# Decoder kernel on one core: who issues the loads of the row maxima, when the class rows are stored, and where the router products stand

## The chip, the cores and the metric

The kernel runs on one core of one Trainium2 chip. The metric is the device time of one execution in microseconds (us); three executions of the kernel before are given, and one more was recorded by the hardware profiler.

## The reference

The program is a two-layer decoder on x of 4 batches x 512 tokens x 128 channels (16 heads of 8 channels). Each line adds a block's output to x:

```python
x = x + L0_attn(_layernorm(x), ...)                  # rwkv, a scan
x = x + L0_xattn(_layernorm(x), ctx_1024, ...)
x = x + L0_ffn(_layernorm(x), ...)                   # causal attention + FFN, and experts
x = x + L1_attn(_layernorm(x), ...)                  # attention with relative positions
x = x + L1_xattn(_layernorm(x), ctx_1024, ...)
x = x + L1_ffn(_layernorm(x), ...)                   # grouped attention
```

The change lies in the third and the sixth. In the third:

```python
scores = jnp.einsum('bqhd,bkhd->bhqk', q, k) / np.sqrt(hd)
attn = softmax(where(causal, scores, min)); o = attn @ v
...
probs = softmax(xt @ router_w); topw, topi = top_k(probs, 2)   # 8 experts
moe_out = sum of topw * expert(xt) over the two chosen
```

In the sixth a similarity with a guide vector puts each token in one of two classes, and softmax attention runs over the keys of the query's own class:

```python
sim = (sim - sim.min()) / (sim.max() - sim.min()); pos = sim > 0.9
x_pos = masked_attn(pos); x_neg = masked_attn(~pos)
reg_out = (x_pos[:, :REG] + x_neg[:, :REG]) * 0.5        # the first 5 tokens
tok_out = where(pos, x_pos[:, REG:], x_neg[:, REG:])
```

## The kernel before

The stages follow one another with a barrier between them. `attention_stage` (L518) is called twice: with the tag `da` for the causal attention of the third block (with `gates`, the router's work, woven in) and with `ga` for the grouped attention of the sixth (with `classes` and `front`, the work on classes and on the first tokens). Both go through 16 units of four heads of one batch, and 8 steps each: 128 steps, written out as loops over `step` on each engine. The order on an engine is the order of its code; semaphores are the only link between the engines.

Exact fp32 scores are made from bf16 parts. Queries and keys are split in three bf16 parts (`parts`), written to DRAM (`stacks_dram`, L606) and loaded again in another layout as `qst` and `kst` (L628), for one unit at a time, into one of NBUF = 4 buffers. For batch 0 SP (SyncE) writes and loads by units (`write_quad`, `load_stack`); the other three batches are written whole (`write_parts`, 18 DMAs) before the loads of the units 4 to 15.

In step n:

- PE (TensorE) makes the scores of step n (L730; in `da` L741 adds the causal mask), DVE (VectorE) reduces them to row maxima (L964). At the end of a unit DVE splits the unit's maxima in three bf16 parts (L947 to L953). In step 8u + 9 PE turns them into rows (`turn_maxima`, L750), ACT (ScalarE) copies the rows to `mrows` (`copy_maxima`, L880) and raises `m_ready`, and two DMAs put them below the queries in `qst` (`load_maxima`, L886), so that the maximum is subtracted by the product itself.
- Thirteen steps later (S_LAG) PE makes the transposed scores (`scores_t`, L765), of a new unit u in step 8u + 13 and after `m_loaded`; ACT takes the exponentials (L872); in `da` POOL (GpSimd) clears what the causal mask excludes (L681); three steps later PE multiplies by the values (`values`, L784), and ACT copies a finished unit out (L892).

The score banks form a ring of two, so PE can be two score steps ahead of DVE; the transposed scores have three banks, and L765 waits for ACT's exponentials of the step before.

`gate_programs` holds the router: `route` (L1060) makes 16 products of 128 tokens with the router's weights (L1063; two passes each, so 32 MATMULs), `chain` is DVE's work on them: its first instruction copies the logits out of bank 6 (L1094), the others come from step 24 on. `grouped_front` is the front of `ga`: on DVE it makes the class rows (`rows_made`, L2306 to L2312), and `store_classes` (L2380) stores them in DRAM with four DMAs, waits for these, and `load_classes` (L635) loads them for a unit with four. `registers_pe` (L2145) puts the work on the first tokens in the steps 3 to 12: L2151 turns what POOL has divided by the totals (L2370).

Of the kernel before, what the change touches and what calls it, by code (L numbers as in the profile page):

```python
# [517 lines left out]
def attention_stage(nc, g, tag, xn, wq, wk, wv, group, scale, o, wo, take, patch=None, causal=False, classes=None,  # L518
# [6 lines left out]
    S_LAG, V_LAG = 13, 3  # L525
    GATE_STEP = 24

# [26 lines left out]
    with ExitStack() as ctx:  # L554
# [9 lines left out]
        with ExitStack() as inner:  # L564
# [32 lines left out]
            with nc.Block() as block:  # L597
                @block.sync
                def _(sp):
# [38 lines left out]

                    for u in range(NBUF):
                        write_quad(u)  # L640
                        if u:
                            load_stack(u - 1)
                    load_stack(NBUF - 1)
                    if front:
                        front.store_classes(sp)
                        for u in range(NBUF):
                            load_classes(u)
                    for b in range(1, B):
                        write_parts(b)
                    for u in range(NBUF, QUADS):  # L650
                        load_stack(u)
                        if classes:
                            load_classes(u)
                    for b in range(1, B):
# [30 lines left out]
                def _(pe):  # L685
# [21 lines left out]
                    else:  # L707
                        project()
                        clear_output()
                    if gates:  # L710
                        gates.route(pe)
                    pe.wait_ge(left, 2 * B)
# [98 lines left out]
                    for step in range(ALL_STEPS):  # L811
                        t = step - S_LAG
                        if step < STEPS:
                            scores(step)
                        if 0 <= t < STEPS:
                            scores_t(t)
                        if causal and step < STEPS:
                            mask_scores(step)
                        if step % 8 == 1 and step // 8 - 1 in turn_slot:
                            turn_maxima(step // 8 - 1)  # L820
                        if 0 <= t - V_LAG < STEPS:
                            values(t - V_LAG)
                        if front and step < S_LAG:
                            front.registers_pe(pe, step)
                        if front and step == S_LAG - 1:
                            clear_output()
                        if step in OUT_STEP:
                            output(OUT_STEP[step])
                        if step in JOIN_STEP:
                            join(JOIN_STEP[step])  # L830
                        if gates and step == S_LAG:
                            pe.wait_ge(gates.copied, 1)
# [8 lines left out]
                def _(act):  # L841
# [40 lines left out]

                    def load_maxima(u):
                        act.wait_ge(m_ready, u + 1)
                        for par in range(2):
                            act.dma_start(qst[64 * par + KS:64 * par + KT, u % NBUF, :, :],  # L886
                                          mrows[6 * par:6 * par + 6, u % 2, :]).then_inc(m_loaded[u % 2], 16)

# [8 lines left out]
                    for step in range(ALL_STEPS):  # L897
                        t = step - S_LAG
                        if front and step < S_LAG:
                            front.registers_act(act, step)  # L900
                        if 0 <= t < STEPS:
                            exponentials(t)
                        if step % 8 == 1 and step // 8 - 1 in turn_slot:
                            copy_maxima(step // 8 - 1)
                            load_maxima(step // 8 - 1)
                        if gates and step == GATE_STEP + 6:
                            gates.exp(act)
                        p = t - V_LAG
                        if p >= 0 and p % 8 == 7:
                            copy_output(p // 8)  # L910
# [10 lines left out]
                def _(dve):  # L921
# [33 lines left out]
                    chain = gates.chain(dve) if gates else None  # L955
                    if gates:
                        next(chain)
                    for step in range(STEPS):
                        u, r = divmod(step, 8)
                        pr, qt = divmod(r, 4)  # L960
                        if gates and step >= GATE_STEP:
                            next(chain, None)
# [77 lines left out]
class gate_programs:  # L1040
# [18 lines left out]

    def route(self, pe):  # L1060
        pe.wait_ge(self.g.weights_loaded[3], 16)
        for n in range(self.tiles):
            last = self.nc.tensor.matmul(self.logits[:, n, :], self.xn[:, n // QT, bass.ts(n % QT, 128)],  # L1063
                                         self.g.w("router"), start=True, stop=True)
        last.then_inc(self.routed, 1)
# [23 lines left out]
    def chain(self, dve):  # L1089
        nc, p, hot1, hot2, rank, most = self.nc, self.p, self.hot1, self.hot2, self.rank, self.most  # L1090
        spread = most[:, :].unsqueeze(2).broadcast_to([128, self.tiles, E])
        order = self.g.c("order").unsqueeze(1).broadcast_to([128, self.tiles, E])
        dve.wait_ge(self.routed, 1)
        nc.vector.tensor_copy(p[:, :, :], self.logits).then_inc(self.copied, 1)  # L1094
# [945 lines left out]
class grouped_front:  # L2040
# [339 lines left out]
    def store_classes(self, sp):  # L2380
        sp.wait_ge(self.rows_made, 6)
        for b in range(B):
            sp.dma_start(self.rows_dram[:, b, :], self.rows[32 * b:32 * b + 1, :, :]).then_inc(self.rows_stored, 16)
        sp.wait_ge(self.rows_stored, 16 * B)

# [147 lines left out]
```

## Time and profile before

| | us |
|---|---|
| median of 3 runs | 1348.95 |
| lowest, highest | 1347.19, 1350.35 |
| the profiled execution's own time | 1349.48 |
| its span, first to last instruction | 1347.8 |
| busy PE, DVE, ACT, POOL | 1129.5, 833.1, 730.6, 331.8 |
| mean granted clock of TensorE, as a share of 2.4 GHz | 0.931 |
| stage `da`, from its first stack write to its last output copy | 196.7 to 402.6 |
| stage `ga`, from its first stack write to the last add | 1099.1 to 1341.5 |

The table gives the profiled execution's numbers unless it says otherwise. In the rows below a time is in us from the span's start, `ACTq` and `SPq` are the instructions that issue DMAs, `x2` after a row says how many instructions it merges, and in brackets stand the engine's idle time before it and what ended it (`issue`: nothing that the profile shows). `L886` is line 886 of the kernel printed above.

### The profile page before, as it was taken

How to read it: one execution, taken by the hardware profiler on the slowest of the kernel's cores; microseconds unless marked ns; L12 is line 12 of the kernel's file. 1: busy time of each engine (PE TensorE's matmuls, PEld its weight loads, DVE VectorE, ACT ScalarE, POOL GpSimd, SP SyncE). 2: the span in 40 equal slices, each digit the busy share in tenths (PEclk: the TensorE clock that was granted, in tenths of full speed). 3: DMA queues.
4: the chain of work that ended last, by engine and by line, in shares of the span. 5: the costliest groups of instructions: out<-in, count | busy, mean ns of one | idle time of the engine just before them, and what ended most of it. 6: DMA issues, size and time to landing. Idle time of an engine off the chain costs nothing. (4 is left out here: it accounts for less than half of the span.)

```text
span 1347.8 us, 35730 instructions
## 1 busy us (share of the span) xinstructions
PE 1129.5 (84%) x14748; PEld 565.2 (42%) x14748; DVE 833.1 (62%) x1316; ACT 730.6 (54%) x1439; POOL 331.8 (25%) x664
## 2 busy tenths in 40 slices
PE   5987788777777999568999999999978866888886
PEld 2332333323323444235766666766745333222221
DVE  3997136766653333336776776776736366888884
ACT  4201453666653222546676676776754362788884
POOL 1543021333320333014422324222204413000000
PEclk8998776999997999779999999999999887899999
DMA  4000007111005330033102102010110022311100
GB/s 179 1 0 0 1 21 227 39 39 38 27 3 105 82 62 1 0 120 41 11 8 17 9 8 18 9 11 7 10 8 1 0 54 90 120 39 39 39 15 32
DMA packets 134480, 51.62 MB, mean 38 GB/s; under 512 B 103904, under 2 KB 126448, under 8 KB 133680
## 3 DMA queue, kind: packets, MB, share of 16 engines
q1 hardware_dynamic: 133744, 48.95, 15.5%
q8 instruction: 118, 1.93, 0.6%
q10 hardware_dynamic: 576, 0.39, 0.1%
q14 instruction: 42, 0.34, 0.1%
HBM read 33.12 MB, written 15.81 MB: 36 GB/s over the span
## 5 line engine op out<-in xcount | busy, mean ns | idle before, releaser
L1952 DVE TENSOR_REDUCE re_nmax<-ps 128x1 f32<-128x512 f32 x256 | 159.0, 684 | 88.6 <-PE ps L1720 88.6
L1863 ACT ACTIVATE re_p<-ps,re_nmax 128x512 f32<-128x512 f32 x256 | 158.9, 688 | 89.9 <-DVE re_nmax L1952 89.9
L964 DVE TENSOR_REDUCE ga_nmax<-ps 128x2 f32<-128x1024 f32 x128 | 149.8, 1219 | 28.4 <-PE ps L730 28.3
L872 ACT ACTIVATE ga_pt<-ps 128x512 f32<-128x512 f32 x256 | 139.2, 598 | 38.3 <-issue 22.0
L1741 PE MATMUL ps<-const,re_p 128*128 128x128 f32 x1024 | 145.3, 281 | 8.0 <-ACT re_p L1863 5.2
L964 DVE TENSOR_REDUCE da_nmax<-ps 128x2 f32<-128x256 f32 (+3 forms) x128 | 103.7, 822 | 46.9 <-PE ps L741 45.3
L872 ACT ACTIVATE da_pt<-ps 128x512 f32<-128x512 f32 (+3 forms) x256 | 97.6, 438 | 60.8 <-PE ps L765 35.4
L1741 PEld LDWEIGHTS ps<-const,re_p 128*128 128x128 f32 x1024 | 108.8, 141 | 36.7 <-ACT re_p L1863 25.3
L1869 ACT ACTIVATE re_pT<-ps 128x512 f32<-128x512 f32 x128 | 76.3, 597 | 28.2 <-PE ps L1741 19.7
L784 PE MATMUL ps<-ga_pt,ga_v 128*9 128x256 f32 x1024 | 81.4, 386 | 10.1 <-ACT ga_osum L892 10.1
L1972 DVE COPY re_pT<-ps 128x512 f32<-128x512 f32 x128 | 82.3, 685 | 10.2 <-PE ps L1741 9.4
L1235 DVE TENSOR_TENSOR ex_u<-ps,ex_s 128x512 f32<-128x512 f32 x48 | 33.2, 691 | 89.6 <-PE ps L1208 89.6
L681 POOL TENSOR_SCALAR_AFFINE_SELECT da_pt<-da_pt 128x256 f32<-128x256 f32 x128 | 52.8, 412 | 143.3 <-ACT da_pt L872 141.8
L1221 ACT ACTIVATE ex_s<-ps 128x512 f32<-128x512 f32 x48 | 28.7, 597 | 94.1 <-PE ps L1208 94.1
L1710 PE MATMUL ps<-re_keys,re_qbd 32*128 32x512 f32 x512 | 73.0, 640 | 0.0
L1629 POOL TENSOR_TENSOR re_keys<-re_k,vec 128x64 f32<-128x64 f32 (+1 forms) x60 | 17.4, 289 | 225.8 <-PE ps L1720 225.8
L1642 POOL TENSOR_TENSOR re_qrel<-re_qd,const 128x64 f32<-128x64 f32 x256 | 68.5, 299 | 11.8 <-DMA re_qd<-re_q_scratch 11.8
L1788 PE MATMUL ps<-re_pT,re_v_far 128*9 128x128 f32 x1536 | 65.6, 285 | 2.7 <-ACT re_near L1875 1.7
L1248 POOL TENSOR_TENSOR ex_u<-ex_u,ex_gates 128x512 f32<-128x512 f32 x32 | 40.4, 1264 | 109.1 <-DVE ex_u L1235 71.5
L730 PE MATMUL ps<-ga_kst,ga_qst 50*128 50x512 bf16 x256 | 51.8, 404 | 13.0 <-DMA ga_kst<-gr_rows_scratch 6.5
L765 PE MATMUL ps<-ga_qst,ga_kst 53*128 53x512 bf16 x256 | 49.9, 386 | 13.4 <-ACT ga_pt L872 12.4
L1208 PE MATMUL ps<-ff_xn,weights 128*128 128x512 f32 x128 | 60.2, 592 | 0.0
(390 smaller groups left out, 1993.3 us busy)
## 6 DMA issues: line engine op xcount, KB each, us to landing
ex_gates<-gates_scratch SPq DMA_DIRECT2D x4, 2048.0 KB, 14.4
da_qst<-da_stacks SPq DMA_DIRECT2D x32, 96.0 KB, 2.3
da_kst<-da_stacks SPq DMA_DIRECT2D x32, 96.0 KB, 2.3
ga_qst<-ga_stacks SPq DMA_DIRECT2D x32, 96.0 KB
ga_kst<-ga_stacks SPq DMA_DIRECT2D x32, 96.0 KB
da_stacks<-da_qkparts SPq DMA_DIRECT2D x6, 384.0 KB, 3.3
ga_stacks<-ga_qkparts SPq DMA_DIRECT2D x6, 384.0 KB, 2.9
weights<-in_weights SPq DMA_DIRECT2D x1, 2048.0 KB, 8.0
```

The costliest lines, as they stand in the source:

```text
L784: last = nc.tensor.matmul(g.ps[32 * j:32 * j + HD + 1, O_BANK, lo:hi], v9[:, QT * b + kt, 4 * quad + j, :], pt[:, (4 * u + kt) % SLOTS, j, ...
L872: nc.scalar.activation(pt[:, (4 * u + kt) % SLOTS, 2 * pr + par, q0:T], g.ps[:, ST_BANK + (2 * t + par) % ST_BANKS, q0:T], ACT.Exp)\
L964: nc.vector.tensor_reduce(nmax[:, u % 2, :, pr, qt], g.ps[:, score_bank[step]:score_bank[step] + 2, 0:keys_of(qt)], AX.X, ALU.max, negate= ...
L1208: last = nc.tensor.matmul(g.ps[:, 2 * m + n % 2, :], g.w(w)[:, bass.ts(f, 128)], x[:, b, :], start=True, stop=True).then_inc(up, 1)
L1642: nc.gpsimd.tensor_tensor(qrel[:, m, pair, :, :, :, two], qd[:, b % 2, OCT * at:OCT * at + OCT, 4 * pair:4 * pair + 4].unsqueeze(2) .broad ...
L1710: nc.tensor.matmul(g.ps[:, S_BANK + quad, :], qbd[rows, m, :, :, :].rearrange("p o h c -> p (o h c)"), keys[rows, b % 2, m, :], start=True ...
L1741: last = nc.tensor.transpose(g.ps[:, bank_of("tile", s, idx), bass.ts(kt, 128)], p[:, QUAD_ORDER[idx], bass.ts(kt, 128)], g.c("ident"))
L1788: last = nc.tensor.matmul(far_out[32 * j:32 * j + HD + 1, :], values, weights, start=kt == 0, stop=kt == QT - 1)
L1863: nc.scalar.activation(p[:, QUAD_ORDER[idx], :], g.ps[:, S_BANK + QUAD_ORDER[idx], :], ACT.Exp, bias=nmax[:, s % 2, idx:idx + 1]).then_inc ...
L1869: nc.scalar.activation(pT_of(s, QUAD_ORDER[idx]), turned_of(s, idx), ACT.Identity)\
L1952: nc.vector.tensor_reduce(nmax[:, s % 2, idx:idx + 1], g.ps[:, S_BANK + quad, :], AX.X, ALU.max, negate=True).then_inc(maxed, 1)
L1972: nc.vector.tensor_copy(pT_of(s, QUAD_ORDER[idx]), turned_of(s, idx)).then_inc(dve_pT, 1)
```

## The change

Three things are changed.

1. `load_maxima`: the two DMAs of unit 0 stay on ACT, those of the units 1 to 15 are issued by SP, each ahead of the load of the stack three units on. This is in both `da` and `ga`.
2. In `ga` the class rows are stored behind the load of stack 0 instead of behind that of stack 3, the wait for the stores stands apart (`wait_stored`) behind the load of stack 1, and the class rows of the units 0 and 1 are loaded there.
3. In `da` the router products are made two in each of the first eight steps, behind the step's mask, instead of all ahead of step 0; DVE copies the logits in step 10 instead of ahead of step 0.

```diff
+                    def load_maxima(u):
+                        sp.wait_ge(m_ready, u + 1)
+                        for par in range(2):
+                            sp.dma_start(qst[64 * par + KS:64 * par + KT, u % NBUF, :, :],
+                                         mrows[6 * par:6 * par + 6, u % 2, :]).then_inc(m_loaded[u % 2], 16)
+                    write_quad(0)
+                    write_quad(1)
+                    load_stack(0)
                     if front:
                         front.store_classes(sp)
-                        for u in range(NBUF):
+                    write_quad(2)
+                    load_stack(1)
+                    if front:
+                        front.wait_stored(sp)
+                        load_classes(0)
+                        load_classes(1)
+                    write_quad(3)
+                    for u in range(2, NBUF):
+                        load_stack(u)
+                        if classes:
                             load_classes(u)
                     for b in range(1, B):
                         write_parts(b)
-                    for u in range(NBUF, QUADS):
-                        load_stack(u)
-                        if classes:
-                            load_classes(u)
+                    for u in range(1, QUADS):
+                        load_maxima(u)
+                        if u + NBUF - 1 < QUADS:
+                            load_stack(u + NBUF - 1)
+                            if classes:
+                                load_classes(u + NBUF - 1)
...
-                    if gates:
-                        gates.route(pe)
...
+                        if gates and step < ROUTE_STEPS:
+                            gates.route(pe, step)
...
-                            load_maxima(step // 8 - 1)
+                            if step // 8 == 1:
+                                load_first_maxima()
...
-                        if gates and step >= GATE_STEP:
+                        if gates and (step == LOGIT_STEP or step >= GATE_STEP):
...
-        for n in range(self.tiles):
+        for n in range(2 * step, 2 * step + 2):
```

ROUTE_STEPS is 8, LOGIT_STEP 10 and GATE_STEP 24 as before.

On SP, in `da`, the stacks of the units 4 and 5 before:

```order
L628 DMA da_qst<-da_stacks 48x2x512 x2
L628 DMA da_kst<-da_stacks 48x2x512 x2
L628 DMA da_qst<-da_stacks 48x2x512 x2
L628 DMA da_kst<-da_stacks 48x2x512 x2
```

and with the change:

```order
L642 DMA da_qst<-da_mrows 3x2x512 x2
L628 DMA da_qst<-da_stacks 48x2x512 x2
L628 DMA da_kst<-da_stacks 48x2x512 x2
L642 DMA da_qst<-da_mrows 3x2x512 x2
L628 DMA da_qst<-da_stacks 48x2x512 x2
L628 DMA da_kst<-da_stacks 48x2x512 x2
```

The loads of the maxima of the units 1 and 2 now stand between the stacks; those of the units 13 to 15 follow the last stack. On ACT nothing stands any more between the copy of the rows and the next exponentials, but for unit 0.

On SP, in `ga`, from the load of stack 1 on before (`gr_rows` are the class rows, `gr_rows_scratch` their place in DRAM):

```order
L628 DMA ga_qst<-ga_stacks 48x2x512 x2
L628 DMA ga_kst<-ga_stacks 48x2x512 x2
L628 DMA ga_qst<-ga_stacks 48x2x512 x2
L628 DMA ga_kst<-ga_stacks 48x2x512 x2
L2383 DMA gr_rows_scratch<-gr_rows 4x1x512 x4
L635 DMA ga_qst<-gr_rows_scratch 2x2x512 x2
L635 DMA ga_kst<-gr_rows_scratch 2x2x512 x2
```

and with the change, from the load of stack 0 on:

```order
L628 DMA ga_kst<-ga_stacks 48x2x512 x2
L2396 DMA gr_rows_scratch<-gr_rows 4x1x512 x4
L606 DMA ga_stacks<-ga_qkparts 32x3x512
L606 DMA ga_stacks<-ga_qkparts 32x2x512
L606 DMA ga_stacks<-ga_qkparts 32x512
L606 DMA ga_stacks<-ga_qkparts 32x1536
L606 DMA ga_stacks<-ga_qkparts 32x1024
L606 DMA ga_stacks<-ga_qkparts 32x512
L628 DMA ga_qst<-ga_stacks 48x2x512 x2
L628 DMA ga_kst<-ga_stacks 48x2x512 x2
L635 DMA ga_qst<-gr_rows_scratch 2x2x512 x2
L635 DMA ga_kst<-gr_rows_scratch 2x2x512 x2
```

Ahead of unit 0's class rows there is now one write of a unit's parts and one stack less, and the last write and the stacks 2 and 3 come behind. The first excerpt shows the stacks 2 and 3 ahead of the stores.

On PE, in `da`, the first steps before:

```order
L702 MATMUL ps<-da_zero 128x512
L1063 MATMUL ps<-weights,ff_xn 128x8 x16
L730 MATMUL ps<-da_kst,da_qst 128x128 x2
L741 MATMUL ps<-loweredb,identb 32x128 x8
L730 MATMUL ps<-da_kst,da_qst 128x256 x2
L741 MATMUL ps<-loweredb,identb 32x128 x8
```

and with the change:

```order
L716 MATMUL ps<-da_zero 128x512
L742 MATMUL ps<-da_kst,da_qst 128x128 x2
L753 MATMUL ps<-loweredb,identb 32x128 x8
L1076 MATMUL ps<-weights,ff_xn 128x8 x2
L742 MATMUL ps<-da_kst,da_qst 128x256 x2
L753 MATMUL ps<-loweredb,identb 32x128 x8
L1076 MATMUL ps<-weights,ff_xn 128x8 x2
```

The sixteen products stand in eight pairs, one pair behind each of the masks of the steps 0 to 7.

## Rows read from the trace of the kernel before

**Rows 1.** The waits: engine, line, waited for; us in total, times, longest.

```profile
ACT da_pt L872 <- issue: 23.5, 15, 1.6
ACT ga_pt L872 <- issue: 22.0, 14, 1.6
```

**Rows 2.** The timeline of one unit of `ga` (unit 9's maxima): start, length, what.

```profile
1245.37 1.49 ACTq L886 DMA_DIRECT2D ga_qst<-ga_mrows  x2
1245.40 0.38 PE L765 MATMUL ps<-ga_qst,ga_kst 53*128 53x512 bf16 x2
1245.61 2.36 DVE L964 TENSOR_REDUCE ga_nmax<-ps 128x2 f32<-128x1024 f32 x2 [0.49 <-PE ps L730]
...
1246.91 6.61 ACT L872 ACTIVATE ga_pt<-ps 128x512 f32<-128x512 f32 x12 [1.56 <-issue]
...
1247.56 0.39 PE L765 MATMUL ps<-ga_qst,ga_kst 53*128 53x512 bf16 x2 [0.91 <-ACT ga_pt L872]
...
1248.86 4.62 DVE L964 TENSOR_REDUCE ga_nmax<-ps 128x2 f32<-128x1024 f32 x4 [0.90 <-PE ps L730]
```

**Rows 3.** The timeline of one unit of `da`.

```profile
304.88 0.27 PE L765 MATMUL ps<-da_qst,da_kst 51*128 51x256 bf16 x2
305.00 1.51 ACTq L886 DMA_DIRECT2D da_qst<-da_mrows  x2
...
306.56 1.15 ACT L872 ACTIVATE da_pt<-ps 128x256 f32<-128x256 f32 x4 [1.59 <-issue]
...
307.00 0.23 PE L765 MATMUL ps<-da_qst,da_kst 51*128 51x128 bf16 x2 [1.07 <-ACT da_pt L872]
...
307.50 1.56 DVE L964 TENSOR_REDUCE da_nmax<-ps 128x2 f32<-128x1024 f32 x2 [1.11 <-PE ps L741]
...
308.91 0.38 PE L765 MATMUL ps<-da_qst,da_kst 51*128 51x512 bf16 x2
```

**Rows 4.** Windows in that unit: length; busy us by engine; PEclk; DMA share; GB/s.

```profile
307.10:307.30 0.20, 0.20 (x14) 0.15 (x16) 0.00 (x0) 0.15 (x2) 0.02 (x1) 1.00 0.09 31
```

**Rows 5.** The timeline of `da`: the maxima of unit 0 and who waits.

```profile
218.10 2.10 ACTq L886 DMA_DIRECT2D da_qst<-da_mrows  x2
...
222.17 0.61 PE L765 MATMUL ps<-da_qst,da_kst 51*128 51x512 bf16 x2 [1.37 <-DMA da_qst<-da_mrows]
```

**Rows 6.** The timeline of the start of `ga`.

```profile
1117.52 0.38 PE L2142 MATMUL ps<-gr_rows,gr_ones 1*128 1x512 bf16 x1
...
1118.43 2.50 SPq L2383 DMA_DIRECT2D gr_rows_scratch<-gr_rows  x4
...
1122.28 3.12 POOL L2370 TENSOR_SCALAR ga_osum<-ga_osum,gr_total 128x512 f32<-128x512 f32 x2
1122.68 0.56 SPq L635 DMA_DIRECT2D ga_kst<-gr_rows_scratch  x2
...
1124.45 1.03 PE L730 MATMUL ps<-ga_kst,ga_qst 50*128 50x512 bf16 x4 [6.55 <-DMA ga_kst<-gr_rows_scratch]
...
1128.11 1.11 PE L2151 MATMUL ps<-const,ga_osum 128*128 128x128 f32 x4
```

**Rows 7.** The timeline of the start of `da`.

```profile
203.20 0.90 SPq L628 DMA_DIRECT2D da_kst<-da_stacks  x2
...
204.09 3.63 PE L1063 MATMUL ps<-weights,ff_xn 128*128 128x8 f32 x32
...
207.66 0.23 PE L730 MATMUL ps<-da_kst,da_qst 48*128 48x128 bf16 x2
...
216.79 0.58 PE L750 MATMUL ps<-identb,da_mparts 128*12 128x128 bf16 x4 [0.61 <-DVE da_nmax L964]
```

**Rows 8.** The page's list of DMAs: what, issuer, count, KB each, us to landing.

```profile
da_kst<-da_stacks SPq DMA_DIRECT2D x32, 96.0 KB, 2.3
```

**Rows 9.** Windows at the start of `da`: length; busy PE, PEld, DVE, ACT, POOL; PEclk; DMA.

```profile
206.00:208.00 2.00, 2.00 (x26) 1.85 (x25) 0.23 (x1) 0.00 (x0) 0.00 (x0) 1.00 0.48 117
...
210.00:212.00 2.00, 1.29 (x24) 0.42 (x27) 1.84 (x3) 0.00 (x0) 0.00 (x0) 0.50 0.68 173
```

More of the change, by code:

```diff
@@ L525, in attention_stage @@
     S_LAG, V_LAG = 13, 3
-    GATE_STEP = 24
+    GATE_STEP, ROUTE_STEPS, LOGIT_STEP = 24, 8, 10
     def first_query(kt):
@@ L637, in load_classes @@
                                     .then_inc(stack_loaded[at], 16)
-                    for u in range(NBUF):
[L640 to L643, printed above, removed]
+                    def load_maxima(u):
[6 more added lines that the diff above has]
+                    load_stack(0)
                     if front:
                         front.store_classes(sp)
-                        for u in range(NBUF):
+                    write_quad(2)
[8 more added lines that the diff above has]
+                        if classes:
                             load_classes(u)
@@ L881, in copy_maxima, with load_first_maxima @@
                             .then_inc(m_ready, 1)
-                    def load_maxima(u):
-                        act.wait_ge(m_ready, u + 1)
+                    def load_first_maxima():
+                        act.wait_ge(m_ready, 1)
                         for par in range(2):
-                            act.dma_start(qst[64 * par + KS:64 * par + KT, u % NBUF, :, :],
-                                          mrows[6 * par:6 * par + 6, u % 2, :]).then_inc(m_loaded[u % 2], 16)
+                            act.dma_start(qst[64 * par + KS:64 * par + KT, 0, :, :], mrows[6 * par:6 * par + 6, 0, :])\
+                                .then_inc(m_loaded[0], 16)
                     def copy_output(u):
@@ L955, in _ @@
                     chain = gates.chain(dve) if gates else None
-                    if gates:
-                        next(chain)
                     for step in range(STEPS):
@@ L1058, in clear, with route @@
         self.nc.gpsimd.memset(self.kept[:, :, :], 0.0).then_inc(self.cleared, 1)
-    def route(self, pe):
+    def route(self, pe, step):
         pe.wait_ge(self.g.weights_loaded[3], 16)
-        for n in range(self.tiles):
+        for n in range(2 * step, 2 * step + 2):
             last = self.nc.tensor.matmul(self.logits[:, n, :], self.xn[:, n // QT, bass.ts(n % QT, 128)],
@@ L1092, in chain @@
         order = self.g.c("order").unsqueeze(1).broadcast_to([128, self.tiles, E])
-        dve.wait_ge(self.routed, 1)
+        dve.wait_ge(self.routed, 8)
         nc.vector.tensor_copy(p[:, :, :], self.logits).then_inc(self.copied, 1)
@@ L2383, in store_classes, with wait_stored @@
             sp.dma_start(self.rows_dram[:, b, :], self.rows[32 * b:32 * b + 1, :, :]).then_inc(self.rows_stored, 16)
+    def wait_stored(self, sp):
         sp.wait_ge(self.rows_stored, 16 * B)
```

## The prediction

> **What bounds the kernel now.** I read the waits of the whole run first, then the timeline of one settled unit of each attention stage, then the starts of the two stages. Nothing outside these stages is touched, so only their length counts.
>
> In the waits the reader is to see a kind that no engine causes: 15 times in `da` and 14 times in `ga`, ACT stands for up to 1.6 us ahead of its exponentials with the releaser "issue" [rows 1]. The timelines show what it is. ACT issues the two DMAs of the maxima itself, which takes 1.49 us, and only then goes on, though the transposed scores it works on next were there [rows 2]. In `ga` they end at 1245.40 + 0.38 = 1245.78 and ACT starts at 1246.91. The delay goes round: PE's next transposed scores wait 0.91 us for ACT, with them in PE's order the next scores, and DVE waits 0.90 us for those. In `da` it is the same chain [rows 3]: scores ready at 305.15, ACT starts at 306.56, PE waits 1.07, DVE 1.11. So each unit is a loop through ACT, PE and DVE, and the issue time is a link of it.
>
> At the start of `ga` PE has nothing to do for 6.55 us [rows 6]: its front ends at 1117.90, and step 0 waits for the class rows, which SP stores only after all four stacks, at 1118.43. At the start of `da` the router products fill PE for 3.63 us, and step 0 follows at 207.66 [rows 7].
>
> **Part 1, the loads of the maxima.** ACT loses two issues per unit for the units 1 to 15 of both stages.
>
> In `ga` ACT can start at about 1245.83 in place of 1246.91. The first half of the pair takes about 0.55 (6.61 / 12), so PE's next L765 can run at 1246.5 in place of 1247.56, and the scores behind it come 1.05 earlier. DVE can use 0.90 of that [rows 2]: it was idle for 0.90 ahead of 1248.86 and then has no gap left there. The 0.49 ahead of 1245.61 stays, because there the two-bank ring makes PE wait for DVE. So DVE bounds the unit next, and the gain is **0.9 us** per unit.
>
> In `da` ACT can start at 305.2. Its first 256-column exponential takes 0.29 (1.15 / 4), so L765 could run at 305.5 but stands behind the scores of step 3, which PE makes up to about 305.85: 1.1 earlier than 307.00. DVE is busy until 306.39 and had a gap of 1.11 [rows 3], so it follows by 1.1, and everything behind hangs on this. **1.1 us** per unit.
>
> The units 2 to 14 are settled: 13 x 0.9 = 11.7 and 13 x 1.1 = 14.3. Unit 1 runs while the start is not yet over; I give it 0.5 in each stage. Unit 15's load is made in the tail, where ACT's gap lies beside PE's join of finished batches: nothing. Sum 27.0.
>
> What the issues cost on SP: SP has no work between the stack loads, its load of stack u + 3 is due three steps behind `m_ready`, so it isn't held up, and the next maxima come a unit later. The only new limit is the landing. In `da` the maxima are ready at 304.97, and L765 of the new unit would want them 1.1 earlier than 308.91, at 307.8: 2.8 us. On ACT's queue the second DMA was issued at 305.75 and its last packets ran in the window up to 307.30 [rows 4]: 1.5 us behind its issue. On SP an issue from SBUF takes between 0.43 (0.90 / 2 of a stack load [rows 7]) and 0.6 us (2.50 / 4 of a class store [rows 6]), so the second stands at 305.4 to 305.6 and lands at 307.1, or 307.5 with some time for the semaphore. It fits by 0.3 to 0.7 us; I charge 0.
>
> The Trainium skill, "DMA: Bandwidth & Descriptors", section "Anatomy of one DMA", gives about 2.0 us fixed for a DMA (for GpSimd's path). With that the landing would be at 307.6 and the term still 1.1; the trace's 1.5 us is shorter, so it goes by the trace.
>
> What is queued behind: the maxima of unit 1 now come behind the 18 writes of the batches 1 to 3. Unit 0's maxima, which travel beside these writes, take 4 us from issue to use and make PE wait 1.37 [rows 5]. That row is the bound for unit 1: nothing, or once 1.4 per stage. They are issued when the writes are nearly through; I take 0.
>
> **Part 2, the class rows in `ga`.** SP now stores them when DVE has made them, and unit 0's rows are issued behind one write of a unit (6 DMAs at 0.5, so 3 us) and one stack load (1.8, twice the 0.90 of [rows 7]) instead of behind all stacks. They then land at about 1118.5, close to PE's readiness at 1117.90, against 1124.45: 5.9 earlier. Not all of it counts. Step 3 turns what POOL divides, and POOL's first division starts at 1122.28 and takes 3.12 / 2 = 1.56 [rows 6], so L2151 can't run before 1123.9, whatever PE does. It ran at 1128.11. **4.2 us**; behind it the work on the first tokens sets the pace as before. Bounds: 3 to 5.9.
>
> **Part 3, the router in `da`.** Stack 0's last DMA is issued at 203.65 and takes 2.3 us [rows 7, 8], so step 0 could start at 206.0 in place of 207.66: 1.7 earlier. But 32 MATMULs move into the steps. At full clock they took 3.63 us, 0.45 per step, which fits beside DVE's reductions. The rows show the clock at 1.00 of 2.4 GHz while PE works without a gap on the router, and at 0.50 (1.2 GHz) right after, in the first steps [rows 9]. At half clock a pair costs up to 0.9. Steps there take PE 0.65 to 0.95 without it (the scores and the mask), so with it about 1.7, against 0.3 to 1.2 of DVE: PE becomes the bound. Steps 0 to 2 end at 209.1, five more take 8.5, and with the rest of step 8 and 9 `turn_maxima` comes at about 219.1 instead of 216.79 [rows 7]. The maxima of unit 0, for which PE waits at 222.17, are later by the same. I charge **+2.3 us**. Bounds: the full clock throughout gives -1.7 to -5 (the wait of 1.37 goes too, and the slow steps behind it are fast), a whole extra spell of slow clock +5. DVE's copy in step 10 falls in its idle time.
>
> **Sum.** -27.0 - 4.2 + 2.3 = -28.9 us. Against the profiled execution's 1349.48 that is 1320.6 with a span of 1318.9; that execution lies 0.5 above the median of the runs shown, so the forecast is 1320 us.
>
> **The rivals.**
>
> *The router is cheap.* If the first steps of `da` run at the full clock, the start gives 1.7 to 5 instead of costing 2.3: 1320 - 5.5 = 1314. For it: PE is kept denser than before. Against: the clock fell while PE was 2.00 of 2.00 us busy with the router [rows 9]. 18%.
>
> *The clock stays up in `ga`.* PE's gap of 6.5 us shrinks to about one. L2151 took 1.11 for four at 0.5 [rows 6]; the first pass over the first tokens would be shorter by about a us, the early steps by another: 1318. The Trainium skill, "TensorE: Matmul & The Clock Gate", section "HAM oscillation", has idle gaps between bursts as what brings the clock down. 12%. This case's trace agrees in `ga`, not in `da` [rows 9], where there was no gap.
>
> *Another link bites first.* The replay takes the rest of each unit as it was. In `ga` it leaves DVE only 0.49 us idle in a unit [rows 2], so PE or ACT may well hold it up somewhere; if a unit gains half, or unit 1's maxima stall both stages, 13 to 16 us are missing: 1334. 15%.
>
> *The other side: the maxima come too late in every unit.* SP's queue carries the stacks, too. In `da` a landing beyond 2.8 us behind `m_ready` eats the gain one for one, and at 3.9 it is gone. Counting `ga` the same way at most (its steps are longer), a landing at 5.0 us costs 1.1 and up to 1.3 per unit instead of gaining 1.1 and 0.9: 13 x 4.4 = 57 more than forecast, so 1377. It decides from 3.9 to 4.0 us, where the 2.9 us gained elsewhere are used up as well. For it: 4 us was seen once, under full DMA load [rows 5]. Against: the settled units have no such load, and 1.5 us was seen there [rows 4]. 3%.
>
> **How the numbers follow.** Forecast 52%, the router cheap 18%, the clock up 12%, half the gain 15%, late maxima 3%. The range leaves out the late maxima, the worst of half the gain and the best sums of the favourable cases: 1311 to 1335. 0.2% of this kernel is 2.7 us, about what a measurement can tell from no change; every case but the last is far beyond it. Faster 0.95, same 0.02, slower 0.03.
>
> **What the changed profile would show.** Right: no wait for "issue" ahead of L872 but at unit 0; in `ga` 10.65 us from one unit's maxima to the next in place of 11.55, DVE's 0.90 gone and its 0.49 left; in `da` 9.3 in place of 10.4; step 0 of `ga` at about 1118.5 less what the earlier stages gained, L2151 about 5 us behind it and right behind POOL's first division; in `da` the first `turn_maxima` about 2.3 later and PE without gaps in the steps 3 to 7. Wrong: a wait for the DMA of `mrows` at L765 in settled units, a unit of `da` above 9.9, or PE idle in the first steps of `da` because the pairs of router products run at full clock.

## The result and the profile after

The kernel after took 1315.02 us (median of 4, 1314.07 to 1316.15), the kernel before 1349.47 beside it: a ratio of 0.9748, 95% interval 0.9731 to 0.9765, so 34 us faster (31.7 to 36.3). Measured a second time beside other kernels (below) the ratio was 0.9775 (0.9748 to 0.9803), 30 us. The forecast was 1320, 29 us faster. The kernel before itself had medians from 1345.7 to 1349.5 in the four comparisons, so kernels of different comparisons are set against each other by their ratios.

In the code after, the lines are shifted: the scores are L742, the mask L753, `turn_maxima` L762, the transposed scores L777, the exponentials L886, the copy of the maxima L894, DVE's reduction L977, SP's maxima L642, ACT's L900 (unit 0 alone), the router L1076, the class rows' store L2396, POOL's division L2383 and the turn of its result L2164.

In the list of waits of the kernel after, no row is left in which ACT waits for "issue" ahead of its exponentials ([rows 1]: 23.5 and 22.0 us). ACT now waits for PE:

```profile
ACT da_pt L886 <- PE ps L777: 43.3, 80, 5.0
ACT ga_pt L886 <- PE ps L777: 21.3, 33, 1.9
```

The timeline of a settled unit of `ga`, as in [rows 2]:

```profile
1218.29 1.47 SPq L642 DMA_DIRECT2D ga_qst<-ga_mrows  x2
1218.41 0.38 PE L777 MATMUL ps<-ga_qst,ga_kst 53*128 53x512 bf16 x2
1218.62 6.88 DVE L977 TENSOR_REDUCE ga_nmax<-ps 128x2 f32<-128x1024 f32 x6 [0.49 <-PE ps L742]
...
1218.84 6.62 ACT L886 ACTIVATE ga_pt<-ps 128x512 f32<-128x512 f32 x12 [0.57 <-PE ps L777]
...
1219.50 0.38 PE L777 MATMUL ps<-ga_qst,ga_kst 53*128 53x512 bf16 x2
```

ACT starts 0.05 us behind the end of the transposed scores (1218.41 + 0.38 = 1218.79) instead of 1.13, PE's next L777 has no wait, and DVE goes through six reductions without a gap. Its 0.90 is gone and its 0.49 is left, as forecast. But the six reductions take 6.88 together, where 2.36 and 4.62 stood in [rows 2]: 6.98. Two reductions that follow at once overlap by 0.1, two with a gap between them don't, so closing a gap gives the gap and 0.1 more. The period of the unit is 10.55 instead of 11.55.

The same in `da`, as in [rows 3]:

```profile
300.06 0.28 PE L777 MATMUL ps<-da_qst,da_kst 51*128 51x256 bf16 x2
300.17 1.47 SPq L642 DMA_DIRECT2D da_qst<-da_mrows  x2
...
300.38 0.66 ACT L886 ACTIVATE da_pt<-ps 128x256 f32<-128x256 f32 x2 [0.23 <-PE ps L777]
...
300.61 2.42 DVE L977 TENSOR_REDUCE da_nmax<-ps 128x2 f32<-128x768 f32 x3 [1.02 <-PE ps L753]
...
302.76 0.28 PE L742 MATMUL ps<-da_kst,da_qst 48*128 48x256 bf16 x2 [0.50 <-DVE da_nmax L977]
302.88 0.38 PE L777 MATMUL ps<-da_qst,da_kst 51*128 51x512 bf16 x2
```

DVE's 1.11 is gone, and 0.96 + 1.56 have become 2.42. The period is 9.20 instead of 10.38.

Where the time went, from the starts of single rows of the two profiled executions. "Copies" are ACT's copies of the maxima, L880 before and L894 after:

| stretch | before | after | difference | forecast |
|---|---|---|---|---|
| start to ACT's last copy of the values in `da` | 205.13 | 206.08 | +1.0 | 0 |
| from there to the first copy of `da` | 12.35 | 14.88 | +2.5 | +2.3 |
| to the second | 11.65 | 11.89 | +0.2 | 0 |
| to the third (unit 1) | 10.82 | 9.94 | -0.9 | -0.5 |
| to the last (units 2 to 14) | 137.05 | 120.83 | -16.2 | -14.3 |
| to the end of `da` (start of DVE's last copy) | 24.93 | 24.82 | -0.1 | 0 |
| to the last product of `ga`'s front | 715.59 | 712.95 | -2.6 | 0 |
| to the first copy of `ga` | 23.17 | 20.47 | -2.7 | -4.2 |
| to the second | 11.63 | 11.26 | -0.4 | 0 |
| to the third (unit 1) | 11.55 | 10.69 | -0.9 | -0.5 |
| to the last (units 2 to 14) | 150.01 | 137.00 | -13.0 | -11.7 |
| to the start of the last add | 26.82 | 26.56 | -0.3 | 0 |

The sum is -33.4, the difference of the spans (1347.8 and 1314.4; both end 7.05 us behind the start of the last add). The first and the seventh stretch are not the change's: no kernel below touches the 716 us between the stages, and over all the profiled executions they took between 711.7 and 717.2.

### The profile page after: what moved, and what is told of

Its sections match the earlier page's. It is cut to its first block and busy times, and to the rows that moved or that the text cites. A ratio compares the mean times of both kernels' runs of the same rounds, so it can differ in the third digit from the quotient of the medians.

```text
span 1314.4 us, 35730 instructions
## 1 busy us (share of the span) xinstructions
PE 1119.4 (85%) x14748; PEld 565.8 (43%) x14748; DVE 830.0 (63%) x1316; ACT 730.3 (56%) x1439; POOL 331.7 (25%) x664
## 5 line engine op out<-in xcount | busy, mean ns | idle before, releaser
L977 DVE TENSOR_REDUCE ga_nmax<-ps 128x2 f32<-128x1024 f32 x128 | 148.3, 1217 | 13.0 <-PE ps L742 12.9
L886 ACT ACTIVATE ga_pt<-ps 128x512 f32<-128x512 f32 x256 | 139.2, 598 | 23.0 <-PE ps L777 21.3
L977 DVE TENSOR_REDUCE da_nmax<-ps 128x2 f32<-128x256 f32 (+3 forms) x128 | 102.7, 821 | 36.0 <-PE ps L753 34.7
L886 ACT ACTIVATE da_pt<-ps 128x512 f32<-128x512 f32 (+3 forms) x256 | 97.5, 438 | 44.4 <-PE ps L777 43.3
L1234 ACT ACTIVATE ex_s<-ps 128x512 f32<-128x512 f32 x48 | 28.7, 597 | 92.7 <-PE ps L1221 92.7
L796 PE MATMUL ps<-da_pt,da_v 128*9 128x256 f32 (+1 forms) x768 | 54.2, 352 | 6.4 <-ACT da_osum L906 6.4
L742 PE MATMUL ps<-ga_kst,ga_qst 50*128 50x512 bf16 x256 | 50.8, 396 | 7.7 <-DVE ga_nmax L977 7.0
```

The lines of the kernel that those rows point to most:

```text
L742: last = nc.tensor.matmul(g.ps[:, score_bank[step] + par, 0:keys], qst[rows, u % NBUF, pr, bass.ts(qt, 128)], kst[rows, u % NBUF, pr, 0:ke ...
L796: last = nc.tensor.matmul(g.ps[32 * j:32 * j + HD + 1, O_BANK, lo:hi], v9[:, QT * b + kt, 4 * quad + j, :], pt[:, (4 * u + kt) % SLOTS, j, ...
L886: nc.scalar.activation(pt[:, (4 * u + kt) % SLOTS, 2 * pr + par, q0:T], g.ps[:, ST_BANK + (2 * t + par) % ST_BANKS, q0:T], ACT.Exp)\
L977: nc.vector.tensor_reduce(nmax[:, u % 2, :, pr, qt], g.ps[:, score_bank[step]:score_bank[step] + 2, 0:keys_of(qt)], AX.X, ALU.max, negate= ...
```

## The start of the two stages after

`ga`, as in [rows 6]:

```profile
1101.39 0.39 PE L2155 MATMUL ps<-gr_rows,gr_ones 1*128 1x512 bf16 x1
...
1102.51 0.61 PE L742 MATMUL ps<-ga_kst,ga_qst 50*128 50x512 bf16 x4 [0.73 <-DMA ga_kst<-gr_rows_scratch]
...
1104.25 2.26 POOL L2362 TENSOR_TENSOR ga_qkparts<-ga_rest,ga_qkparts 128x512 bf16<-128x512 f32 x2 [7.47 <-issue]
...
1106.51 6.20 POOL L2383 TENSOR_SCALAR ga_osum<-ga_osum,gr_total 128x512 f32<-128x512 f32 x4
...
1108.13 1.12 PE L2164 MATMUL ps<-const,ga_osum 128*128 128x128 f32 x4 [2.11 <-POOL ga_osum L2383]
```

Against the front's last product, step 0 comes 1.12 us behind instead of 6.93: 5.8 earlier, 5.9 forecast. L2164 comes 6.74 behind instead of 10.59, 3.9 earlier, and waits for POOL's first division, as forecast. What follows took longer than before, though: 13.73 us from L2164 to the first copy, against 12.58. The clock shows why. Windows of the kernel after (length; busy PE, PEld, DVE, ACT, POOL; PEclk; DMA share; GB/s):

```profile
1106.00:1108.00 2.00, 0.02 (x2) 0.00 (x0) 1.68 (x2) 0.00 (x0) 2.00 (x2) 0.50 0.52 134
...
1116.00:1118.00 2.00, 2.00 (x10) 0.98 (x9) 1.06 (x1) 0.30 (x2) 0.46 (x1) 0.51 0.72 272
1118.00:1120.00 2.00, 1.65 (x12) 1.06 (x10) 1.86 (x6) 0.75 (x2) 0.00 (x0) 1.00 0.00 0
```

PE was granted 1.2 GHz from 3 to 16.5 us behind the start of the front's last product, in both kernels. The work on the first tokens now starts earlier and lies deeper in this spell.

`da`, as in [rows 7] and the end of [rows 5]:

```profile
207.03 0.23 PE L742 MATMUL ps<-da_kst,da_qst 48*128 48x128 bf16 x2 [1.81 <-DMA da_kst<-da_stacks]
...
210.85 1.02 PE L1076 MATMUL ps<-weights,ff_xn 128*128 128x8 f32 x4
...
220.27 0.59 PE L762 MATMUL ps<-identb,da_mparts 128*12 128x128 bf16 x4 [0.51 <-DVE da_nmax L977]
...
225.89 0.61 PE L777 MATMUL ps<-da_qst,da_kst 51*128 51x512 bf16 x2 [1.62 <-DMA da_qst<-da_mrows]
```

The stage began 0.95 later in this execution. Without that, step 0 is 1.6 earlier, and the first maxima are turned at 219.3 (219.1 forecast, 216.79 before). A step's four router MATMULs take 0.61 in the steps 0 to 2, at the full clock, and 1.02 in the slow steps 3 to 7, where PE has no gap.

## The experiments

The result was 5 us better than the forecast, and two theories say why. **Theory A**: the mechanisms are the forecast's, and the sizes are those of the table above (per unit 1.00 us in `ga` and 1.18 in `da` in place of 0.9 and 1.1); the three parts add up. **Theory B**: the forecast's sizes are right, and the missing 5 us come from somewhere else. Each experiment opens with what was expected of it.

**Each part alone, and the change without part 3.** The first three put one part of the diff on the kernel before, the fourth leaves part 3 away:

```diff
 p1_maxima (on the kernel before)
-                            load_maxima(step // 8 - 1)      # act
+                            if step // 8 == 1:
+                                load_first_maxima()         # act
+                        load_maxima(u)                      # sp, ahead of load_stack(u + NBUF - 1)
 p2_classes (on the kernel before)
+                    load_stack(0)
+                    if front:
+                        front.store_classes(sp)
+                    write_quad(2)
 p3_router (on the kernel before)
-                    if gates:
-                        gates.route(pe)
+                        if gates and step < ROUTE_STEPS:
+                            gates.route(pe, step)
```

The cuts are short: p2_classes has the whole new order of SP's issues that part 2 describes, and p3_router makes DVE copy the logits in step 10. p12_no_router is the full change with the edit of p3_router turned round.

> Part 1 alone: the maxima of the units 1 to 15 issued by SP, the rest as before. Theory A (the unit's loop was closed by the issue, and the profile after shows its full size): 0.99 us less per settled unit of ga, 1.19 in da, 0.9 for unit 1 of each; -27.3 for the 13 + 13 settled units, -1.7 for the two units 1, and with the spell of slow clock that some of the units of da had about -30. Ratio 0.978. Theory B (the prediction's sizes, 0.9 and 1.1, and the missing 5 us come from another part): -27, ratio 0.980, and the periods in the trace are 10.65 and 9.3. If the surplus came from the sum of several parts (interaction through the clock), periods as in B here but shorter in the full change.

Measured: ratio 0.9787 (0.9764 to 0.981), 28.7 us faster (25.6 to 31.8). The interval holds the ratios of both theories, the trace tells them apart: units 2 to 14 of `da` took 121.04, of `ga` 136.95, nearly the numbers of the full change. These are the periods of theory A, without help from another part.

> Part 2 alone: the class rows stored behind the first stack's load, the rest as before. Theory A (what the profile after shows): step 0 of ga 5.8 us earlier against the last product of the front, L2151 3.9 earlier behind POOL's first division, and only 2.7 left at the first copy of the maxima because PE runs at 1.2 GHz for longer behind it: -2.7, ratio 0.998. Theory B (the prediction): -4.2 all the way, ratio 0.9969. Rival (clock stays up in ga): -6, 0.9955.

Measured: 0.9968 (0.9953 to 0.9983), 4.3 us (2.3 to 6.3). In its trace step 0 comes 1.29 us behind the front, the turn of POOL's result (L2151 before) 6.54, the first copy 20.27: 2.9 earlier than before. The interval holds all three ratios, that of the rival too, so the time decides nothing; the profiled execution has A's size.

> Part 3 alone: the router's products two tiles per step in the steps 0 to 7 of da. Theory A (prediction and profile after): the first maxima are turned 2.3 to 2.5 us later, and nothing gives that back: +2.5, ratio 1.0019. Rival (the delay is given back within the stage, since a loop closed by the issue on ACT doesn't care, or the slow clock ends sooner): 0. Rival (router cheap): -1.7 to -5.

Measured: 1.0022 (1.0009 to 1.0036), 3.0 us slower (1.2 to 4.8). The first copy of `da` comes 14.73 behind the last copy of the values, 2.4 later than before. Both rivals lie outside the interval.

> The change without part 3: the router's products stay ahead of step 0. Theory A: the parts add up, so this is 2.5 us faster than the full change, 1312.5, ratio 0.973. Rival (in the faster loop the start of da no longer counts, or router cheap): equal to the full change, 1315, or slower by 1.7.

Measured: 1312.74, ratio 0.9738 (0.9702 to 0.9774); alone this can't be told from the full change. Its trace had a surprise at the start of `ga`. Windows of this kernel, whose front ended 1.5 us later than that of the kernel after:

```profile
1108.00:1110.00 2.00, 1.54 (x6) 0.82 (x6) 0.92 (x1) 0.39 (x1) 2.00 (x3) 0.50 0.50 152
1114.00:1116.00 2.00, 1.64 (x13) 1.12 (x11) 1.56 (x3) 0.75 (x2) 0.00 (x0) 1.00 1.10 397
```

and of the kernel after at the same times:

```profile
1108.00:1110.00 2.00, 1.72 (x7) 0.89 (x7) 0.17 (x1) 0.60 (x1) 2.00 (x3) 0.50 0.48 142
1114.00:1116.00 2.00, 1.85 (x10) 1.72 (x8) 1.42 (x2) 0.23 (x1) 0.00 (x0) 0.50 1.09 398
```

The full clock was back 10.7 us behind the start of the front's last product instead of 16.5, and the first copy came at 18.1 instead of 20.5. Nothing of `ga` differs between the two kernels.

**One of two loads stays on ACT.** In the full change:

```diff
-                        for par in range(2):      # load_maxima on sp
+                        for par in range(1):
+                        for par in range(0 if u == 0 else 1, 2):   # act, for every unit
+                            act.dma_start(...)
```

> The full change, but of the two loads of a unit's maxima SP issues one and ACT the other (units 1 to 15). ACT keeps 0.75 us of the 1.49. Theory A (the issue is a link of the unit's loop, so that the gain is in proportion to the time that it is away from ACT, up to the gap of DVE): ga starts 0.33 us of the 1.08 late, which leaves about 0.75 to 0.85 of the 0.99; da 0.75 of 1.18; 13 x (0.2 + 0.43) = 8 us slower than the full change, 1323, ratio 0.981. Rival (what counts is that ACT is held at all, or the semaphores of the pair): the gain is gone, 1343. Rival (one issue hides in ACT's slack): 1315.

Measured: 1322.28 us, ratio 0.9822 (0.9791 to 0.9853), which leaves out both rivals (1343 and 1315 would be 0.998 and 0.977). Its unit of `ga`:

```profile
1222.62 0.73 ACTq L900 DMA_DIRECT2D ga_qst<-ga_mrows  x1
1222.64 0.38 PE L777 MATMUL ps<-ga_qst,ga_kst 53*128 53x512 bf16 x2
1222.85 7.12 DVE L976 TENSOR_REDUCE ga_nmax<-ps 128x2 f32<-128x1024 f32 x6 [0.49 <-PE ps L742]
...
1223.39 6.61 ACT L886 ACTIVATE ga_pt<-ps 128x512 f32<-128x512 f32 x12 [0.80 <-PE ps L777]
...
1224.05 0.39 PE L777 MATMUL ps<-ga_qst,ga_kst 53*128 53x512 bf16 x2 [0.15 <-ACT ga_pt L886]
```

The periods are 10.80 and 9.62, so 0.25 and 0.42 us above the full change where 0.2 and 0.43 were expected. With 1.49, 0.73 and 0 us of issues on ACT the unit of `da` takes 10.38, 9.62 and 9.20, that of `ga` 11.55, 10.80 and 10.55. The first 0.76 us taken from ACT give 0.76 and 0.75, the other 0.73 give 0.42 and 0.25: the issue time is a link of the loop, and its last 0.3 us in `da` and 0.5 in `ga` are free.

**The maxima late in every unit**, the rival of the other side made real:

```diff
                     for u in range(1, QUADS):
-                        load_maxima(u)
                         if u + NBUF - 1 < QUADS:
                             load_stack(u + NBUF - 1)
...
+                        load_maxima(u)
```

> The full change with the stack's load (and the class rows' in ga) ahead of the maxima in SP's queue. The stack's buffer comes free three steps behind the copy of the maxima, so the maxima are issued about 3.2 to 3.9 us later, and behind 1.7 us of issues (2.8 in ga). Theory A (a maxima landing beyond the 2.8 us of da and about 3 us of ga makes PE wait one for one): a landing about 7 us behind m_ready in da and 8.2 in ga, 4 and 5 us per unit lost, 15 x 9 = 135 us slower than the full change, about 1450. Rival (PE has more room than I counted, because its next work can go ahead of L777): under 1350.

Measured: 1458.7, ratio 1.0839 (1.0791 to 1.0887). Its settled `da`, and a unit of its `ga`:

```profile
308.53 0.78 SPq L628 DMA_DIRECT2D da_qst<-da_stacks  x2
309.36 0.90 SPq L628 DMA_DIRECT2D da_kst<-da_stacks  x2
310.30 1.46 SPq L642 DMA_DIRECT2D da_qst<-da_mrows  x2
313.00 0.43 PE L777 MATMUL ps<-da_qst,da_kst 51*128 51x512 bf16 x2 [3.55 <-DMA da_qst<-da_mrows]
...
1269.58 1.49 SPq L642 DMA_DIRECT2D ga_qst<-ga_mrows  x2
1272.22 0.61 PE L777 MATMUL ps<-ga_qst,ga_kst 53*128 53x512 bf16 x2 [5.20 <-DMA ga_qst<-ga_mrows]
```

The mechanism is real, and one line's place decides it. But the total came near the expected 135 us by luck. The periods become 14.8 and 17.05, 5.6 and 6.5 us longer where 4 and 5 were expected, and only in the 12 units that have a stack's load in front, where 15 were counted: 12 x 12.1 = 145 instead of 15 x 9 = 135. The landing itself was as expected (L777 runs 6.9 us behind `m_ready` in `da`, 8.3 in `ga`). What the expectation left out is the clock. Windows over these units:

```profile
245.00:410.00 165.00, 117.48 (x1644) 38.54 (x1642) 84.38 (x149) 79.40 (x200) 36.26 (x89) 0.75 0.10 29
1200.00:1395.00 195.00, 123.94 (x1124) 27.96 (x1126) 112.83 (x134) 106.94 (x202) 0.00 (x0) 0.79 0.09 26
1270.00:1272.00 2.00, 0.00 (x0) 0.00 (x0) 0.00 (x0) 0.00 (x0) 0.00 (x0) 0.50 0.03 8
```

The granted clock is 0.75 and 0.79 here and 1.00 over the settled units of the kernel after. In `ga` it falls inside PE's long wait of each of these units, as in the last row. That this spell makes up the 1.5 us or so per unit beyond the expectation is likely, but was not tested by itself.

These rows also measure the landing: PE goes on 2.70 and 2.64 us behind the start of the two issues, about 1.9 behind the start of the second, which comes 0.76 later. In the kernel after, PE's weight load of L777 in the unit of `da` shown above:

```profile
302.86 0.10 PEld L777 LDWEIGHTS ps<-da_qst,da_kst 51*128 51x128 bf16 x2
```

The issues start at 300.17, so this is 2.69 behind them, just as in the run order, where PE stood waiting for the landing (weight load at 312.99, issues at 310.30). So in a settled unit of `da` it is the landing that releases L777 in the kernel after, too. It comes as PE gets there, and L777's MATMUL follows at 302.88 without a gap: no slack is left, but no loss is seen either.

**The router's products where PE waits anyway.** In the full change:

```diff
-    GATE_STEP, ROUTE_STEPS, LOGIT_STEP = 24, 8, 10
+    GATE_STEP, LOGIT_STEP = 24, 13
+    ROUTE_AT = {10: (8, 10), 11: (10, 12), 12: (12, 16)}
+                    if gates:
+                        gates.route(pe, 0, 8)     # ahead of step 0
...
-                        if gates and step < ROUTE_STEPS:
-                            gates.route(pe, step)
+                        if gates and step in ROUTE_AT:
+                            gates.route(pe, *ROUTE_AT[step])
```

> The full change with the router's products in other places: 8 of the 16 tiles ahead of step 0, where PE waits 1.8 us for stack 0, the rest in the steps 10, 11 and 12 (2, 2, 4), ahead of PE's wait for unit 0's maxima. Theory A (the price of part 3 is PE's time in the steps 3 to 7, while step 0 comes 1.6 us earlier): step 0 as early as in the full change, the first maxima turned as early as at 10.9 us behind the last copy of the values instead of 14.2, 2.5 to 4 us faster than the full change, 1312, ratio 0.972. Rival (the slow clock makes PE the bound wherever the products stand): no faster than the full change, 1315.

Measured: 1310.28, ratio 0.9731 (0.9701 to 0.9762).

```profile
203.23 1.85 PE L1079 MATMUL ps<-weights,ff_xn 128*128 128x8 f32 x16
...
205.26 0.23 PE L745 MATMUL ps<-da_kst,da_qst 48*128 48x128 bf16 x2 [0.18 <-DMA da_kst<-da_stacks]
...
214.16 0.58 PE L765 MATMUL ps<-identb,da_mparts 128*12 128x128 bf16 x4 [0.61 <-DVE da_nmax L980]
...
218.78 1.88 PE L1079 MATMUL ps<-weights,ff_xn 128*128 128x8 f32 x8
...
220.78 0.64 PE L780 MATMUL ps<-da_qst,da_kst 51*128 51x512 bf16 x2
```

The first half of the products fills the wait for stack 0 (0.18 is left of 1.81), the last ones the wait for unit 0's maxima (none left of 1.62). The first copy comes 10.58 behind the last copy of the values (14.88 in the full change), the second copy 3.3 earlier than there. The trace has what theory A said; the time alone can't show it, since the interval holds 0.9748, the first ratio of the full change.

**The writes of the batches 2 and 3 behind unit 0's maxima**, on the change without part 3:

```diff
-                    for b in range(1, B):
+                    write_parts(1)
+                    load_maxima(0)                # on sp; act's is gone
+                    for b in range(2, B):
                         write_parts(b)
```

> The change without part 3, and the writes of the batches 2 and 3 issued behind unit 0's maxima, which SP now loads too. Theory A (unit 0's maxima land late because they travel beside the 18 writes): PE's wait for them in da, 1.4 to 2.2 us, goes; ga has no such wait and stays; 1.5 to 2 us faster than without this edit, 1311, ratio 0.972. Rival (the landing is late from the 6 writes of batch 1 alone, or the writes come too late for stack 8 and 12): equal, or slower by some us.

Measured: 1314.93, ratio 0.9764 (0.9734 to 0.9794), against 0.9738 and 0.9742 without this edit: no gain, and the wait grew.

```profile
216.89 3.82 SPq L606 DMA_DIRECT2D da_stacks<-da_qkparts  x6
...
220.75 1.67 SPq L642 DMA_DIRECT2D da_qst<-da_mrows  x2
...
223.66 0.61 PE L781 MATMUL ps<-da_qst,da_kst 51*128 51x512 bf16 x2 [2.86 <-DMA da_qst<-da_mrows]
```

The landing was 2.9 us instead of 4.0 to 4.8, so the writes beside it do delay it. The queue isn't the reason: by the traces' records of the semaphore the two loads of a settled unit of `da` were complete 2.7 us behind the first issue from ACT (kernel before) as from SP (kernel after). But SP issues them 2.7 us later, because six writes stand in front of them in its queue; ACT was free at 218.1. Issuing unit 0's maxima on ACT is right.

**The full change and that without part 3 again, and a version with one more edit**: split_pool has the router's products in the places of the run split, and POOL makes two divisions ahead of the two subtractions (L2362) that stood in front of L2164's input. The edit on top of split:

```diff
-        thirds(1)
         for b in range(B):
+            if b == 2:
+                thirds(1)
             pool.wait_ge(self.inverted, b + 1)
```

> The full change a second time, beside the next two kernels. Theory A (the parts alone add up to -30 us and the 34 of the first measurement holds 3 to 4 us of scatter between executions): ratio 0.975 to 0.978. Rival (the parts help each other by 4 us): 0.9748 or less. In its trace the slow clock at the start of ga may be short or long: the time from the front's last product to the first copy of the maxima is 18.1 with a short one and 20.4 with a long one.

> The change without part 3 a second time. Theory A (part 3 costs 2.5 us in the full change too): 2 to 3 us faster than the run beside it of the full change. Rival (part 3 costs 2.5 at the first maxima but gives it back behind them, where PE waits less for unit 0's maxima and unit 1 is shorter): within 1 us of it.

> The router's products in the places of the run split, and in the front of ga POOL makes its first two divisions ahead of the two subtractions of batch 1 (2.26 us), behind which they stood. Theory A (L2164 hangs on POOL's first division: PE waited 2.1 us for it in the profile after): L2164 2.1 us earlier and with it the first steps of ga; 5 to 6 us faster than the full change beside it, ratio 0.971. Rival (the later divisions, now behind the subtractions, or the slow clock of PE set the pace): as fast as split, 3.5 us faster than the full change.

Measured: 1314.22, 0.9775 (0.9748 to 0.9803); 1310.79, 0.9742 (0.9721 to 0.9762); 1308.66, 0.9731 (0.9712 to 0.975). The second measurement of the full change is theory A's, the parts add up; the first (0.9748) was the rival's, and the two intervals overlap. Without part 3 the kernel is 3.4 us faster by the medians, as theory A has it, though these two intervals overlap a little as well. The third has the lowest median of all, 5.6 us below the full change beside it; its ratio is that of split. Its start of `ga`:

```profile
1097.44 3.12 POOL L2387 TENSOR_SCALAR ga_osum<-ga_osum,gr_total 128x512 f32<-128x512 f32 x2 [6.89 <-DVE gr_total L2333]
...
1100.23 1.11 PE L2167 MATMUL ps<-const,ga_osum 128*128 128x128 f32 x4
```

The turn comes 4.21 us behind the start of the front's last product instead of 6.23 in the run split, 2.0 earlier. How much of that reaches the end isn't settled: the two versions' intervals overlap, and in the profiled executions the spell of slow clock was longer here (the clock was back at 14 us, in split at 9.7), with the first copy at 17.94 and 18.02.

## Why the prediction was right, and where a size was off

**Part 1.** Right in mechanism and place: the wait for "issue" went, the 0.90 and 1.11 went, the 0.49 stayed, and the dose of the run half confirms the loop. The mis-sized term is "0.9 us per unit" and "1.1 us": it counted DVE's gap and left out that closing a gap lets two reductions overlap. The settled periods give 1.00 and 1.18; over the 26 units, without the clock's share below, 28.0 us in place of 26.0, so 2.0 more. Unit 1 gave 0.9 in each stage in this profile instead of 0.5; in the `ga` of the other kernels with part 1 in full it gave between -0.8 and 0.9, by whether a spell of slow clock fell in it.

1.2 us more came from the clock, which the prediction used for `ga`'s start and not here. The kernel before had one unit of 11.59 among those of 10.38. Its window, and the same stretch after:

```profile
298.00:300.00 2.00, 2.00 (x22) 0.38 (x14) 0.65 (x2) 1.15 (x3) 0.41 (x1) 0.50 0.54 153
```

```profile
298.00:300.00 2.00, 1.56 (x30) 0.69 (x28) 1.55 (x4) 1.25 (x4) 0.81 (x2) 1.00 0.01 4
```

All three kernels with both issues on ACT (before, part 2, part 3) had such a unit in the settled part of `da`, at three different places. Of the nine kernels in which SP issues at least one of the two in time, none had one. PE is busy 15.20 of 20 us in the window 260 to 280 before and 16.61 after. That the denser PE keeps the clock up is the likely reading; it was not tested by itself.

**The landing.** "It fits by 0.3 to 0.7 us" was too kind. The term taken from the trace, 1.5 us behind the second issue, is the last packet; until PE may go on it is 1.9. The Trainium skill, "DMA: Bandwidth & Descriptors", section "Anatomy of one DMA", has about 2.0 us fixed, for GpSimd's path; these loads were issued by SP, and their 1.9 is near that figure and not near my reading. The charge of 0 was right by a hair, not by the margin that was worked out. "One for one" as the price of lateness was too low: in the run order the landing was some 4 us beyond the 2.8 of `da`, and the unit took 5.6 more, at a lower clock. Its total, 144 us above the full change by the medians, is near the expected 135 only because fewer units paid more each.

**Unit 1 behind the 18 writes:** nothing, as charged; PE loses time to no maxima but unit 0's.

**Part 2.** Right up to L2164: 5.8 for 5.9, 3.9 for 4.2, behind POOL's first division. Over all nine kernels with part 2 whose POOL is unchanged the turn comes 5.6 to 7.0 behind the front, against 10.4 to 10.8 before. The step that failed is "behind it the work on the first tokens sets the pace as before": in five of these nine the clock came back as late as before (16 to 17 us behind the front), in one at 13, and 2.7 to 3.6 us were left at the first copy, the 2.7 of the kernel after below the bound of 3; in three it came back at 9.7 to 10.7, and 5.1 were left. The rival "the clock stays up in `ga`" is thus half right: it never stayed up, but the spell was shorter in some executions. The Trainium skill, "TensorE: Matmul & The Clock Gate", section "HAM oscillation", blames idle gaps between bursts. The run order fits it: PE waits 5.2 us in a late unit of `ga`, and the clock falls inside the wait. The start of `ga` doesn't: with PE's gap cut from 6.55 to 0.73 us the clock fell at the same place, 3 us behind the front. Why is open.

**Part 3.** Right: +2.5 for +2.3 in the trace, +3.0 (1.2 to 4.8) alone, with PE bound in the steps 3 to 7 at the slow clock. A pair of products cost 1.02 there, a little more than the "up to 0.9" of the sum. "The router is cheap" fell, though the time came out near its 1314, which is chance: in the trace the first copy of `da` comes 2.5 us later, not earlier.

**What is left.** The parts alone sum to 28.7 + 4.3 - 3.0 = 30.0, with some 4 us of uncertainty; the full change gave 34 and 30. So between 1 and 5 us were missing in the forecast. The terms named account for 2.0 + 1.2 + 0.8 more and 1.5 less, so 2.5; in the profiled execution the 716 us between the stages add 2.6 and the stretch ahead of `da` takes 1.0 away, which is scatter. It can't be told closer.

## What to carry to other kernels

A wait for "issue" ahead of an engine's work means that its own DMA issues stand in its queue; if that engine is a link of a loop, move them to a queue that is idle at that time, put them ahead of everything in it that waits for a later event, and size the gain by the gap of the engine that bounds next, plus the overlap that closing the gap gives back. Measure a load's landing by when a waiting engine goes on, not by its last packet. Work that "also fits" belongs where the engine waits for a DMA anyway, not where its clock is low.

## What the runs showed of the hardware

- The granted clock of PE in one and the same stretch differs between executions: at the start of `ga` it was back at 2.4 GHz between 9.7 and 16.7 us behind the start of the front's last product, and between the shortest and the longest spell lay 2.4 us at the first copy.
- With waits of 3.5 and 5.2 us in each unit (run order) PE was granted 0.75 and 0.79 of 2.4 GHz over the settled units, with waits of at most 0.7 us (kernel after) 1.00.
- Two reductions of DVE that follow at once take 0.1 us less than two with a gap (6.88 for six, against 2.36 + 4.62).
- A load from SBUF to SBUF of this size lets PE go on 1.9 us behind the start of its issue, from SP's queue in settled units. Beside the writes of the batches 1 to 3 it is longer: PE went on 4.0 to 4.8 us behind the start of unit 0's two issues instead of 2.7, and waited 1.4 to 2.2 us for them.
